# Attention on one core: one maximum instruction for two heads, sums directly behind the values, and causal masking moved to GpSimd

## What is computed

```python
B, S, D = 2, 2048, 512;  H, dk = 16, 32
q, k, v = split_heads(x @ Wq.T), split_heads(x @ Wk.T), split_heads(x @ Wv.T)
q, k = _rope(q), _rope(k)
scores = jnp.einsum('bhqd,bhkd->bhqk', q, k) / math.sqrt(dk)
scores = jnp.where(causal[None, None], scores, -jnp.inf)
attn = jax.nn.softmax(scores, axis=-1)
ctx = jnp.einsum('bhqk,bhkd->bhqd', attn, v)
return ctx.transpose(0, 2, 1, 3).reshape(B, S, D) @ Wo.T
```

## Time and profile before

| | us |
|---|---|
| time of one execution, median of three | 1840.8 |
| profiled execution, span | 1836.8 |
| attention, first score to last | 1170 |
| TensorE busy, whole span | 1737 |
| VectorE / ScalarE / GpSimd busy, whole span | 1167 / 784 / 804 |

### The profile page before, as it was taken

One profiled execution on the slowest core, in us unless ns is written; L12 is line 12 of the kernel. 1 busy time (PEld: TensorE's weight loads), 2 busy tenths in 40 slices (PEclk: granted clock), 3 DMA queues, 4 the chain that ended last, 5 costly groups with the idle time before them and its releaser, 6 DMA issues. The chain is left out here.

```text
span 1836.8 us, 33962 instructions
## 1 busy us (share of the span) xinstructions
PE 1737.2 (95%) x9952; PEld 1010.7 (55%) x9952; DVE 1167.2 (64%) x2630; ACT 784.3 (43%) x1544; POOL 804.4 (44%) x434
## 2 busy tenths in 40 slices
PE   6999995789999999989999998999999996999998
PEld 5888884444444444444445444444444433677776
DVE  6667663687767767657767775776776704566564
ACT  3222221135555545545555554554555563222321
POOL 1333333335655646535655564564664672111211
PEclk9999998599999989989999998999999997999999
DMA  5556545830161161142115006116102003131221
GB/s 172 201 197 220 194 166 174 185 72 24 25 139 25 25 131 33 25 90 70 30 35 124 25 10 137 25 25 135 29 25 71 12 7 101 41 134 69 83 100 47
DMA packets 103259, 157.60 MB, mean 86 GB/s; under 512 B 10544, under 2 KB 43824, under 8 KB 100400
## 3 DMA queue, kind: packets, MB, share of 16 engines
q1 hardware_dynamic: 93296, 136.10, 27.4%
q10 hardware_dynamic: 9792, 19.40, 2.9%
HBM read 96.23 MB, written 58.72 MB: 84 GB/s over the span
## 5 line engine op out<-in xcount | busy, mean ns | idle before, releaser
L771 ACT ACTIVATE a_probs<-a_st 128x512 f32<-128x512 f32 (+3 forms) x1280 | 613.2, 536 | 543.3 <-PE a_st L661 277.7
L618 POOL TENSOR_TENSOR a_pair<-a_probs 128x1024 f32<-128x1024 f32 (+2 forms) x320 | 614.8, 1938 | 396.7 <-ACT a_probs L771 396.7
L790 DVE TENSOR_REDUCE a_part<-a_mx 128x1 f32<-128x512 f32 x768 | 507.7, 684 | 208.8 <-PE a_mx L649 206.8
L649 PE MATMUL a_mx<-a_k_stack,a_q_stack 96*128 96x512 f32 (+3 forms) x1280 | 493.5, 428 | 45.1 <-DMA a_q_stack<-qk_scratch 24.5
L661 PE MATMUL a_st<-a_q_stack,a_k_stack 98*128 98x512 f32 (+3 forms) x1280 | 447.9, 393 | 5.1 <-ACT a_probs L771 2.2
L649 PEld LDWEIGHTS a_mx<-a_k_stack,a_q_stack 96*128 96x128 f32 x1280 | 229.7, 196 | 389.5 <-DVE a_part L790 179.5
L794 DVE CUSTOM_DVE_ANT_0 a_mx<-a_mx,a_mask 128x384 f32<-128x384 f32 (+3 forms) x512 | 250.5, 498 | 140.7 <-PE a_mx L649 138.1
L661 PEld LDWEIGHTS a_st<-a_q_stack,a_k_stack 98*128 98x128 f32 x1280 | 242.8, 193 | 83.6 <-ACT a_probs L771 52.7
L217 POOL TENSOR_TENSOR p_rot<-p_mul 128x1024 f32<-128x1024 f32 x32 | 90.7, 2836 | 213.3 <-DVE p_mul L412 213.3
L675 PE MATMUL a_av<-a_probs,shared 128*32 128x512 f32 (+3 forms) x1280 | 161.7, 551 | 0.7
L675 PE MATMUL a_av<-a_probs,a_v 128*32 128x512 f32 (+3 forms) x1280 | 160.0, 546 | 0.7
(11 more groups left out here) (138 smaller groups left out, 1656.8 us busy)
## 6 DMA issues: line engine op xcount, KB each, us to landing
a_q_stack<-qk_scratch SPq DMA_DIRECT2D x96, 256.0 KB, 4.9
a_k_stack<-qk_scratch SPq DMA_DIRECT2D x21, 1024.0 KB, 13.7
qk_scratch<-p_rot_hi SPq DMA_DIRECT2D x32, 512.0 KB, 3.1
qk_scratch<-p_rot_lo SPq DMA_DIRECT2D x32, 512.0 KB, 3.9
v_scratch<-p_v_st SPq DMA_DIRECT2D x32, 256.0 KB, 6.1
ctx_scratch<-a_ctx_st SPq DMA_DIRECT2D x32, 256.0 KB, 2.4
f_ctx<-ctx_scratch SPq DMA_DIRECT2D x8, 1024.0 KB, 8.9
f_x<-in_x SPq DMA_DIRECT2D x8, 1024.0 KB, 7.8
```

The source lines that it names most:

```text
L618: pool.tensor_tensor(pair[:, p % 2, h:h + 2, q0:TT], probs[:, s % RING, h:h + 2, q0:TT], probs[:, (s + 1) % RING, h:h + 2, q0:TT], ALU.add ...
L649: pe.matmul(mx_ps[k % BANKS][:, 0:width], q_stack[0:96, t, h, qi * P:(qi + 1) * P], k_stack[par][0:96, h, c * TT:c * TT + width], start=Tr ...
L771: act.activation(probs[:, s % RING, h, q0:TT], st_ps[:, (HG * s + h) % BANKS, q0:TT], ACT.Exp, scale=SCORE_SCALE).then_inc(exp_done, 1)
L790: dve.tensor_reduce(out, mx_ps[k % BANKS][:, :], AX.X, ALU.max).then_inc(max_done, 1)
```

## The change

1. An item becomes a pair of heads: two matmuls into two neighbouring banks, and where no mask is needed one VectorE instruction over both, 128x1024 elements to two maxima. On the diagonal VectorE still has one instruction for each head. 160 items become 80, and three buffers of one bank become two of two banks.
2. `a_st` has two banks instead of three.
3. TensorE goes by pairs of steps. In a half pair stand four scores of the step two ahead, an item behind each as far as it has any, then `values` of the half's step; `sums` follows at once behind the second `values` of its pair.
4. The mask matmuls L664 and their two constants are gone. GpSimd instead writes zeros over the later keys of the probabilities of a diagonal step, 128x512 elements in one `affine_select` (`drop_later_keys`), and `values` of such a step waits for it.
5. `values` waits once for all four heads, `sums` once for both halves of the added pair. `a_probs` holds four steps instead of five. The items' plan, SyncE's places for its transfers and VectorE's transposes go by pairs.

```diff
-LAG = 2
-RING = 5
-
-ITEMS = [(t, qi, h, c) for t in range(QT) for qi in range(SUB) for h in range(HG) for c in range(t + 1)]
+RING = 4
+LAST_PAIR = [e // 2 for e in UNIT_END]
+
+ITEMS = [(t, qi, hp, c) for t in range(QT) for qi in range(SUB) for hp in range(HG // 2) for c in range(t + 1)]
...
-        BANKS = 3
+        BANKS = 2
...
-        mx_ps = [ctx.enter_context(nc.psum_tensor(f"a_mx{n}", [P, TT], F32)) for n in range(BANKS)]
+        mx_ps = [ctx.enter_context(nc.psum_tensor(f"a_mx{n}", [P, 2, TT], F32)) for n in range(2)]
...
+            def drop_later_keys(g, s):
+
+                t, j = STEPS[s]
+                q0 = (j - t * SUB) * P
+                block = probs[:, s % RING, :, q0:q0 + P]
+                wait_alone(pool, exp_done, exps(g, s, HG - 1), pool_passed)
+                pool.affine_select(block, block, pattern=[[0, HG], [1, P]], compare_op=ALU.is_ge, fill=0.0, base=0,
+                                   channel_multiplier=-1).then_inc(masked, 1)
...
+                    if j >= t * SUB:
+                        drop_later_keys(g, s)
+                        drop_later_keys(g, s + 1)
+                        pool.wait_ge(masked, diagonal_steps(g, s + 1))
                     pool.wait_ge(pair_done, pairs(g, p - 2))
...
-                pe.wait_ge(exp_done, HG * NSTEP * g + prior_use(n, HG * NSTEP) + 1 + BANKS)
-                mm = pe.matmul(st_ps[:, n % BANKS, q0:TT], k_stack[par][0:98, h, j * P:(j + 1) * P],
-                               q_stack[0:98, t, h, q0:TT], start=True, stop=not diagonal)
-                if diagonal:
-                    mm = pe.matmul(st_ps[:, n % BANKS, q0:q0 + P], eye[:, :], later[:, :], start=False, stop=True)
-                mm.then_inc(st_done, 1)
+                pe.wait_ge(exp_done, HG * NSTEP * g + n + 1)
+                pe.matmul(st_ps[:, n % BANKS, q0:TT], k_stack[par][0:98, h, j * P:(j + 1) * P],
+                          q_stack[0:98, t, h, q0:TT], start=True, stop=True).then_inc(st_done, 1)
...
+                if j >= t * SUB:
+                    pe.wait_ge(masked, diagonal_steps(g, s))
+                else:
+                    pe.wait_ge(exp_done, exps(g, s, HG - 1))
...
+                for p in range(NPAIR):
+                    items = [(n, k) for n, k in items_of_pair(p, first) if not (n and last)]
+                    middle = (len(items) + 1) // 2
+                    for half, due in enumerate((items[:middle], items[middle:])):
+                        s = 2 * p + 2 + half
+                        for i in range(max(HG, len(due))):
+                            if i < HG and s < NSTEP:
+                                scores(g, par, s, i)
+                            elif i < HG and not last:
+                                scores(g + 1, 1 - par, s - NSTEP, i)
+                            if i < len(due):
+                                n, k = due[i]
+                                item(g + n, (par + n) % 2, next_use if n else use, k)
+                        values(g, par, 2 * p + half)
+                    sums(g, p)
...
+                    dve.tensor_reduce(heads_part[:, 2 * hp:2 * hp + 2, qi, c], mx_ps[k % 2][:, :, :], AX.X,
+                                      ALU.max).then_inc(max_done, 1)
```

More of the change, by code:

```diff
@@ L116, in wait_alone @@
     eng.sem_inc(passed, 1)
-def units_ended_at_step(s, first):
-    return [(n, ITEMS[k][0]) for n, k in items_of_step(s, first) if k in ITEM_END]
 class Weights:
@@ L470, in attend @@
         rsum_b = sb("a_rsum_b", [P, TT])
+        ones = sb("a_ones", [P, DK])
         mask = sb("a_mask", [P, TT])
[L472 to L474 removed]
         part = sb("a_part", [P, HG * SUB, QT])
@@ L619, in add_pairs @@
                                            probs[:, (s + 1) % RING, h:h + 2, q0:TT], ALU.add).then_inc(pair_added, 1)
-                    for ahead, t_out in unit_ended_before(s, 1):
-                        if not (ahead and first):
-                            divide(g - ahead, t_out)
+                    for before, t_out in unit_ended_before(p, 1):
+                        if not (before and first):
+                            divide(g - before, t_out)
             def divide(g, t):
@@ L683, in sums @@
                 t, j = STEPS[s]
-                first, last = j == 0, s + 1 in UNIT_END
-                q0 = max(0, j - t * SUB) * P
-                q1 = max(0, j + 1 - t * SUB) * P
-                if first:
+                unit_first, unit_last = j == 0, p in LAST_PAIR
+                q0, q1 = (max(0, j + n - t * SUB) * P for n in range(2))
+                if unit_first:
                     pe.wait_ge(sum_turned, 4 * g + t + START)
-                for h in range(HG):
-                    rows = slice(h * DK, (h + 1) * DK)
-                    if q1 > q0:
-                        pe.matmul(sum_ps[rows, q0:q1], ones[:, :], probs[:, s % RING, h, q0:q1],
-                                  start=first, stop=False, tile_position=(0, h * DK))
@@ L694, in sums @@
-                for h in range(HG):
-                    rows = slice(h * DK, (h + 1) * DK)
-                    if h % 2 == 0:
-                        pe.wait_ge(pair_added, 2 * (NPAIR * g + p) + h // 2 + 1)
-                    mm = pe.matmul(sum_ps[rows, q1:TT], ones[:, :], pair[:, p % 2, h, q1:TT],
-                                   start=first and q1 == q0, stop=last, tile_position=(0, h * DK))
+                if q1 > q0:
+                    for h in range(HG):
+                        pe.matmul(sum_ps[h * DK:(h + 1) * DK, q0:q1], ones[:, :], probs[:, s % RING, h, q0:q1],
+                                  start=unit_first, stop=False, tile_position=(0, h * DK))
@@ L700, in sums @@
+                pe.wait_ge(pair_added, 2 * (NPAIR * g + p) + 2)
+                for h in range(HG):
+                    mm = pe.matmul(sum_ps[h * DK:(h + 1) * DK, q1:TT], ones[:, :], pair[:, p % 2, h, q1:TT],
+                                   start=unit_first and q1 == q0, stop=unit_last, tile_position=(0, h * DK))
                 mm.then_inc(pair_done, 1)
             def group(g, par, use, next_use, first, last):
[L703 to L740 removed]
@@ L742, in _ @@
-            pe.wait_ge(mask_done, 1)
+                for p in range(NPAIR):
+                    items = [(n, k) for n, k in items_of_pair(p, first) if not (n and last)]
[12 more added lines that the diff above has]
+                    sums(g, p)
@@ L743, in _ @@
             for k in range(BEFORE_FIRST):
                 item(0, 0, None, k)
-            pe.wait_ge(consts_done, 2)
             pe.wait_ge(key_ones, 2)
             pe.wait_ge(ones_done, 1)
-            for h in range(HG):
-                scores(0, 0, 0, h)
+            for s in range(2):
+                for h in range(HG):
+                    scores(0, 0, s, h)
             pe.wait_ge(first_values, 2 * 16)
```

207 lines of the change are left out of this document (89 added, 118 removed).

## The result

The changed kernel takes 1889.8 us (median of four runs, 1886.6 to 1897.0) against 1838.9 us: 1.027 times the time, 95% interval 1.021 to 1.032. I had forecast 1790 and a faster kernel. The profiled execution has a span of 1884.6 us.

A forecast was written before the change was run, and what follows sets the result against it. Attention lasts as long as TensorE's queue. Six loop groups -40 us, VectorE's turn -9, first and last group 0, about 1 for `sums`: 1787 for the profiled execution, so 1790; range 20 to 75 us faster, chance 0.62.

The forecast's parts named there:

- the maxima's banks: Two `a_mx` buffers of two banks: TensorE waits for VectorE's reduce only in halves with three items, 3.0 us a group.
- The sign of being wrong: Listed signs: over 0.5 us wait before the fourth score, `values` waiting for a select, clock under 0.95 without TensorE's turn.
- Rival C: TensorE's pauses in nearly every half pair lower its clock, 5 us a fall; one per unit makes 1950 us; chance 0.09.
- The turn of VectorE: VectorE's idle time of 3.71 us at its loop turn, with the clock fall behind it, passes unseen: -9 us.
- rival D: A GpSimd select near its upper bound of 5.9 us makes TensorE follow GpSimd, about 2100 us; chance 0.05.
- the first and the last group together: Attention's first and last head groups: gains and losses within them sum to 0 us.
- the recurrence: 1.42 us from a score to the slot's end of the one reusing its bank; four scores without items take 2.10.
- masks: 64 mask matmuls a group go, at 0.10 us each: -6.4 us a group, bounds -2.6 and -12.
- visits: `sums` directly behind the odd step's `values`, two visits a pair for three: 0.31 us for 20 pairs, -6.2 a group.
- waits of before that go: 8.0 of a group's 143.1 us taken as TensorE's waits for exponentials and banks, gone or priced anew.
- new waits: Waits a group for two score banks, 8.0 and 3.0 us, and for two maxima buffers, 3.0 us.
- rival B: The two score banks cost more and eat the gain: 1825 to 1850 us, no change; chance 0.20.

The follow-up runs named there:

- after_reduce: The changed kernel with the cast and the subtraction of a unit's maxima replaced by four one-input reduces: 1799.4 us, 0.976 of the kernel before.
- before_merged: The kernel before with `sums` directly ahead of `values`, two visits a pair instead of three: 1889.5 us, 1.025 of the kernel before.
- after_masks: after_reduce with the 64 mask matmuls a group in place of the selects on GpSimd: 1835.6 us, 0.996 of the kernel before.
- after_split: after_order with each pair's last score between the odd step's `values` and `sums`, three visits again: 1795.0 us, 0.975 of the kernel before.
- after_order: after_reduce with a half pair's items reordered, two of them between the second and third score: 1764.6 us, 0.958 of the kernel before.
- before_reduce: The kernel before with the cast and the subtraction replaced by the four one-input reduces: 1833.8 us, 0.9945 of the kernel before.

## Why the prediction was wrong, step by step

**The step that failed** is in the sentences on the maxima's banks: "Elsewhere more than 3 us lie between an item and the second one after it. VectorE's work stays near 100 us of 137." They take VectorE's instructions at their durations in the trace of before. I asked of every edit what it does on its own engine, and of the selects whether GpSimd has room; I did not ask which instructions now stand beside each other in time. After the change GpSimd's pair additions fall into the time of the unit's maxima. I put that down to the exponentials, which are issued two steps ahead; no run isolates which part of the new order does it. VectorE's cast and subtraction then take 1.2 to 1.7 and 2.3 us instead of 0.17 and 0.18 (3.2 to 3.7 us more in three of four units); TensorE waits behind them, and the clock falls. Price: 90 us of medians (1889.8 less 1799.4), more than everything the change gains.

None of my rivals had this mechanism. The sign of being wrong that came true is the clock: 0.94 in groups where TensorE has no turn. Rival C had the symptom, a clock that falls in many units at once. Its price of 5 us for a fall was twice too high as a price of the clock: 16 falls went with the collision and 41 us with them, 2.6 us each; only with the waits ahead of them (36.9 us) is it 4.9. And its cause, the short pauses for score banks, is refuted: after_reduce keeps them and loses the falls. Waits of up to 0.46 us, even 13 half pairs in a row, left the clock at 1.00; behind six waits of 1.0 us in before_merged it fell three times, behind 18 of 1.5 to 2.2 us in the changed kernel 16 times.

**What held.** With the collision gone the rest came out near the sum: 1799 for 1790, and 137.7 us for a clean group where I had 136.5. The closeness is in part luck, as the next part shows. The reduce: 1.218 us for 1.22. The turn of VectorE passes unseen: without the collision the clock falls only at TensorE's own two turns, four times before. GpSimd: 0.64 us a select (I had 1.2), and no `values` waited for it; rival D is out. For the first and the last group together I had 0; in after_reduce the first is 1.4 us shorter and the last 4.7 longer. The last group: in its second half every full half pair waits for a score bank,

```profile
1535.56 0.73 PE L665 MATMUL a_st<-a_q_stack,a_k_stack 98*128 98x512 f32 x2
1536.75 0.98 PE L665 MATMUL a_st<-a_q_stack,a_k_stack 98*128 98x512 f32 x2 [0.45 <-ACT a_probs L749]
1537.66 1.06 PE L679 MATMUL a_av<-a_probs,a_v 128*32 128x512 f32 x8
```

four scores in 2.10 us (1535.56 to 1537.66), to the hundredth what the recurrence gave.

**What was mis-sized, and partly cancelled.** For a clean group, from the runs:

| term, us a group | forecast | measured | from |
|---|---|---|---|
| masks | -6.4 | -4.2 | after_masks against after_reduce |
| visits | -6.2 | -3.4 | after_split against after_order |
| waits of before that go | -8.0 | -3.3 | 143.1 - 4.2 - 3.4 = 135.5, against after_order's 132.2 |
| new waits | +14.0 | +5.5 | after_reduce's 137.7 against 132.2 |
| group | 136.5 | 137.7 | after_reduce |

The 8.0 us of waits were a remainder: 143.1 less my sum of slots. TensorE's waits in that group of before, which I hadn't set beside it, list one row:

```profile
PE a_st L661 <- ACT a_probs L771: 0.2, 1, 0.2
```

That row is too little, though: a wait shorter than the matmuls in flight is no idle time in the records. It does show in the distance from one start to the next. Two full-width visits of `values` in that group, the first held up by its step's exponentials, the second not:

```profile
532.11 1.44 PE L675 MATMUL a_av<-a_probs,a_v 128*32 128x512 f32 x8
...
536.20 1.07 PE L675 MATMUL a_av<-a_probs,a_v 128*32 128x512 f32 x8
```

Over the group the slots of `values` add up to 37.9 us before and to 34.7 in after_split, which has as many visits. So 3.2 us were `values` that waited for their own step's exponentials, as I had assumed, and they went. The remaining 4.7 of the 8.0 were work: my slots for scores and maximum matmuls with their edges come to 75.6 us, where the trace of before has 81.7 and that of after_split 82.6 (the masks' own slots, 5.2 us against my 6.4, take 1.2 of it back). No change of banks takes that away. (From the slots that I read, the scores sum to 31.5 us and not 31.8, and the edges to 0.22 a visit and not 0.20; with these the remainder is 7.4.)

So the gains were 9.7 us too large (masks 2.2, visits 2.8, work taken for waits 4.7) and the new waits 8.5 too large. That these nearly cancel, and leave 137.7 beside 136.5, is luck.

That rests on differences between whole kernels; that the terms add up was not measured. The same goes for rival B: the bank waits alone never cost what the change gained, since after_reduce, with all of them, is 2.4% faster than before (up to 0.6 of that may be the reduces' own, by before_reduce).

## What to carry to other kernels

When a change moves work in time, look on both sides for VectorE instructions that take a second read port (by the rule above two SBUF inputs, or a float32 copy) and now fall beside GpSimd's long ones. The size of the small instruction doesn't matter: 128x16 waits until GpSimd's instruction ends, and the next one waits again if GpSimd has another addition ready. Look in the old trace for the one instruction of a group that took ten times its mean and follow who waited behind it; if it can't be moved, a reduce over the same data with one input isn't held.

A remainder is not a measurement. If a sum of slots leaves 8 us, find them in the trace before letting a change remove them: the long ones as rows in the waits, the short ones, which the records hide, as distances between starts.

Count banks in the unit that the work is issued in, and place the long items between the two uses of a short resource: the same instructions in another order gave 35 us here.

## What the runs showed of the hardware that I had not expected

- A VectorE cast of 128x16 (0.17 us alone) takes up to 1.93 us beside a GpSimd addition, a subtraction 2.30; each ends about 0.03 us after GpSimd's instruction. A one-input reduce in the same place takes 0.17 to 0.21. A GpSimd select holds too: a subtraction begun at 1513.72 beside a select from 1513.53 to 1514.18 took 0.49.
- The price isn't linear: one hold of 1.2 us a unit costs 5 to 8 us in the kernel, two in a row 90, since only the second gets past the slack and then, in 16 of 18 places, has a clock fall of 3.4 to 10.2 us behind it.
- VectorE idled 7.9 us and more where it began a turn of its loop in before_merged, twice what the trace of before shows. Why isn't known.
- TensorE's waits of 0.45 us for a bank, in 13 half pairs in a row, did not move its clock.
